# The last block of the scan: statistics in its last chunk, the first tokens' low parts on GpSimd, the first up weights' low part on VectorE, the third gather behind the scan

## The reference

```
xn = layernorm(x)                                # 8192 tokens x 256
# recurrent layer: 8 heads, state 64, head width 64
x1 = silu(causal_conv(xn @ Wx.T)); z = xn @ Wz.T
b = x1 @ Wb.T; c = x1 @ Wc.T; dt = softplus(x1 @ Wdt.T + b_dt)
for t in tokens:                                 # the scan, per head
    state = exp(dt[t] * a) * state + dt[t] * b[t] (x) x1[t]
    y[t] = c[t] . state
y = y + d_param * x1
yn = (y - mean) / sqrt(var + eps) * gn_w + gn_b  # mean, var over tokens
s = (yn * silu(z)) @ Wout.T
# experts: 8, each takes the 1024 tokens with the highest gate
idx = top_k(softmax(xn @ Wr + br).T, 1024)
tokens = xn[idx]
mid = silu(tokens @ Wu + bu); out = mid @ W_down + b_down
ffn = scatter_add(G * out, idx)
```

## Time and profile before

| | us |
|---|---|
| median of 3 runs (1223.07 to 1223.29) | 1223.28 |
| the profiled execution's own time | 1221.26 |
| its span in the trace | 1219.4 |
| VectorE busy in the span | 951.9 (78%) |
| ScalarE busy | 684.5 (56%) |
| GpSimd busy | 792.1 (65%) |

### The profile page before, as it was taken

The page is one execution under the profiler, slowest core; times in us unless marked ns, Lnnn a source line. Parts: engine busy times, 40 slices in busy tenths (PEclk is TensorE's granted clock), DMA queues, the critical chain, the costliest instruction groups (busy, mean ns, idle before and its releaser), DMA issues.

```text
span 1219.4 us, 31280 instructions
## 1 busy us (share of the span) xinstructions
PE 1205.7 (99%) x12203; PEld 1010.9 (83%) x12203; DVE 951.9 (78%) x2027; ACT 684.5 (56%) x1401; POOL 792.1 (65%) x788
## 2 busy tenths in 40 slices
PE   9999999999999999999999999999999999999998
PEld 4666678888888888888888887898899989899998
DVE  7999977898985777777778767987777775777676
ACT  6999985555565465565555556544333332555444
POOL 4889945545555577677776758467766645576674
PEclk9999999999999999999999999999999999999999
DMA  9799764643343343443343435565544446799995
GB/s 300 252 343 347 289 236 141 113 136 122 132 139 118 136 128 121 141 130 117 134 135 122 136 123 172 175 156 97 114 87 105 85 84 130 259 319 325 333 333 166
DMA packets 112354, 214.33 MB, mean 176 GB/s; under 512 B 20432, under 2 KB 78544, under 8 KB 107600
## 3 DMA queue, kind: packets, MB, share of 16 engines
q1 hardware_dynamic: 99056, 195.04, 47.5%
q0 software_dynamic: 12288, 17.05, 8.1%
q10 hardware_dynamic: 864, 0.24, 0.1%
HBM read 131.03 MB, written 81.26 MB: 174 GB/s over the span
## 4 chain that ended last, share of the span: by engine, by line
PE 88%; DVE 5%; ACT 3%; DMA 2%; issue 1%; POOL 1%; SPq 0%; ACTq 0%; DVEq 0%
PE ps L1439 27%; PE ps L1802 11%; PE ps L2061 9%; PE ps L2295 8%; PE ps L2274 7%; PE ps L1520 4%; PE ps L1487 3%; PE ps L1546 3%; PE ps L1509 3%; PE ps L1531 2%; PE ps L1560 2%; PE ps L690 2%; PE ps L743 1%; DMA x_dram<-x 1%; PE ps L1781 1%
## 5 line engine op out<-in xcount | busy, mean ns | idle before, releaser
L1395 ACT ACTIVATE decay<-tap,ncum 128x128 f32<-128x128 f32 x344 | 105.5, 389 | 141.8 <-POOL tap L1289 141.8
L1987 POOL DMA_INDIRECT ffn_dram<-ob,idx x64 | 109.6, 1713 | 85.7 <-DVE ob L1906 71.4
L2023 ACT ACTIVATE mid<-ps,b_up 128x512 f32<-128x512 f32 x96 | 66.0, 689 | 151.2 <-PE ps L1802 139.5
L1296 POOL TENSOR_TENSOR x_lo<-x,x_hi 128x512 fp32r<-128x512 f32 x56 | 78.0, 1392 | 104.1 <-ACT x_hi L1368 104.1
L1174 DVE TENSOR_TENSOR x_dt<-ps,dt 128x512 f32<-128x512 f32 x64 | 44.3, 692 | 117.8 <-PE ps L1546 117.6
L1439 PE MATMUL ps<-x_hi,w_hi_b 128*128 128x512 f32 x240 | 99.5, 414 | 0.0
L1439 PE MATMUL ps<-x_hi,w_hi_c 128*128 128x512 f32 x240 | 99.3, 414 | 0.0
L2150 POOL TENSOR_SCALAR yc<-yc,gn_scale,gn_shift 128x512 f32<-128x512 f32 x56 | 77.2, 1390 | 31.2 <-DMA yc<-y_dram 31.2
L1439 PE MATMUL ps<-x_lo,w_hi_b 128*128 128x512 f32 x240 | 94.4, 393 | 0.0
L1439 PE MATMUL ps<-x_lo,w_hi_c 128*128 128x512 f32 x240 | 94.2, 393 | 0.0
L1439 PE MATMUL ps<-x_hi,w_lo_c 128*128 128x512 f32 x240 | 93.7, 390 | 0.0
(11 more groups left out here) (319 smaller groups left out, 4075.9 us busy)
## 6 DMA issues: line engine op xcount, KB each, us to landing
tap<-cum_dram SPq DMA_DIRECT2D x43, 512.0 KB
x_dram<-x SPq DMA_DIRECT2D x16, 1024.0 KB, 5.7
yc<-y_dram SPq DMA_DIRECT2D x16, 1024.0 KB, 6.8
y_dram<-yb SPq DMA_DIRECT2D x30, 512.0 KB
x<-x_dram SPq DMA_DIRECT2D x26, 512.0 KB, 3.8
cum_row<-cum_dram SPq DMA_DIRECT2D x21, 512.0 KB
rows_dram<-xn SPq DMA_DIRECT2D x16, 512.0 KB, 3.3
ffn_dram<-zero SPq DMA_DIRECT2D x64, 128.0 KB
```

Of the source, the lines that this page charges most:

```text
L1296: nc.gpsimd.tensor_tensor(low, raw, high, ALU.subtract).then_inc(x_lo_ready, 1)
L1395: n = nc.scalar.activation(decay[g % 2][:, h, :], cum_row[g % NR][:, row, :], ACT.Exp, bias=t.ncum[:, g, h:h + 1])
L1987: pool.indirect_dma_start(out=t.ffn_dram, out_offset=bass.IndirectOffsetOnAxis(ap=t.idx[:, e, h * HC + c:h * HC + c + 1], axis=0), in_=ob[ ...
```

## The change

It moves steps between engines and places; the arithmetic is the same, but for one more copy.

- Statistics: of the block before the last, one quarter was taken in chunk 61, one in 62 and two in 63; now all four in chunk 63, before the two `x.middle` steps.
- Token tile 0: ScalarE copies each half to `mid` too, and GpSimd (`token_lo_early(pool, 0)`) forms the low part. The first copies of tile 1 now wait for it half by half (`xg_lo_ready`), since they overwrite `mid`. ScalarE's four copies of tile 0 move ahead of `exp_rows(62)`; those of tile 1 are split, half 0 ahead of `decays(62)`, half 1 at the end of chunk 61.
- The up weights' high part moves to chunk 59 on ScalarE, and their low part from GpSimd to VectorE at the end of chunk 59.
- GpSimd: `causal(62)`, `decay_c(61)`, low part of tile 0, then `causal(63)`, `decay_c(62)`, low part of tile 1, `decay_c(63)`.
- The third gather goes from chunk 63 to the start of the expert stage on GpSimd, behind a wait for the third up slice.

```diff
--- before
+++ after
...
@@ -1164,8 +1164,6 @@
             last = g % SPAN == SPAN - 1
             if g >= LAST:
                 sums(g - 1)
-            if g == LAST + 1:
-                x.token_lo(dve, 0)
             dve.wait_ge(x_turned, g + 1)
             until(dve, y_mm, g)
             if g > LAST:
@@ -1195,14 +1193,16 @@
                 next_bits(g - 1)
             if LIST0 - 1 <= g < LIST1 - 1:
                 list_slots(g - LIST0 + 1)
-            for m in range(c, c + 1) if 0 < b < NB - 1 else ((), (0,), (1,), (2, 3))[c] if b else ():
+            for m in range(c, c + 1) if 0 < b < NB - 1 else ((), (), (), range(MT))[c] if b else ():
                 dve.wait_ge(y_ready, CH * b)
                 v.bn_stats(t.ystat[:, b - 1, m, :], yb[(b - 1) % 2][:, m, :]).then_inc(stat_done, 1)
             if SLOTS <= g < SLOTS + CH:
                 slots(c)
             elif LIST1 < g <= LIST1 + 2:
                 read_lists(g - LIST1 - 1)
-            if g == NT - 1:
+            if g == LAST - 1:
+                x.split_up_lo(dve, v, 0)
+            elif g == NT - 1:
                 for f in range(2):
                     x.middle(dve, 0, f)
 
@@ -1339,19 +1339,18 @@
             b, c = g // CH, g % CH
             if g <= LAST:
                 causal(g + 1)
-            if g % SPAN and g != LAST + 2:
+            if g % SPAN and g not in (LAST + 1, LAST + 2):
                 decay_c(g)
             if LAST - 2 <= g < LAST:
                 x.gather(pool, *x.passes[g - LAST + 2])
             elif g == LAST:
-                x.split_up_lo(pool, nc.gpsimd, 0)
                 causal(g + 2)
+                decay_c(g + 1)
+                x.token_lo_early(pool, 0)
             elif g == LAST + 1:
-                x.token_lo_early(pool)
+                causal(g + 2)
                 decay_c(g + 1)
-                causal(g + 2)
-            elif g == NT - 1:
-                x.gather(pool, *x.passes[2])
+                x.token_lo_early(pool, 1)
             if b + 2 < NB:
                 lo_part(b + 2, c)
             if b + 1 < NB:
@@ -1403,10 +1402,8 @@
             if g == 0:
                 b_part(b + 1, c)
                 exp_rows(1)
-            if g == LAST:
-                x.split_up_hi(act, 0)
-            elif g == LAST + 1:
-                x.token_hi(act, 1)
+            if g == LAST + 1:
+                x.token_hi(act, 1, (0,))
             if g + 1 < NT:
                 decays(g + 1)
             if b + 2 < NB:
@@ -1414,14 +1411,18 @@
             if b + 1 < NB:
                 if g:
                     b_part(b + 1, c)
+            if g == LAST - 1:
+                x.split_up_hi(act, 0)
+            elif g == LAST:
+                x.token_hi(act, 0)
             if b + 1 < NB and c == CH - 1:
                 c_part(b + 1, c)
             if g + 2 < NT and (g + 2) % SPAN:
                 exp_rows(g + 2)
             if b + 1 < NB and c < CH - 1:
                 c_part(b + 1, c)
-            if g == LAST:
-                x.token_hi(act, 0)
+            if g == LAST + 1:
+                x.token_hi(act, 1, (1,))
 
     @block.tensor
     def _(pe):
@@ -1717,25 +1718,29 @@
     def split_up_hi(act, g):
         act.wait_ge(up_loaded[g % 2], 32 * (g // 2 + 1))
         if g == 0:
-            act.wait_ge(t.c_ready, MT * (s.NB - 1))
+            act.wait_ge(t.b_ready, MT * (s.NB - 1))
         elif g >= 2:
             act.wait_ge(up_mm, NH * FT * GS * (g - 1))
         nc.scalar.activation(up_hi[g % 2][:, :, :], up_raw[:, :, :], ACT.Copy).then_inc(up_hi_ready, 1)
 
     def split_up_lo(eng, engine, g):
         eng.wait_ge(up_hi_ready, g + 1)
+        if g == 0:
+            eng.wait_ge(t.c_ready, MT * (s.NB - 1))
         engine.tensor_tensor(up_lo[g % 2][:, :, :], up_raw[:, :, :], up_hi[g % 2][:, :, :].bitcast(F32),
                              ALU.subtract).then_inc(up_lo_ready, 1)
 
-    def token_hi(act, u):
+    def token_hi(act, u, parts=range(KT)):
         if u == 0:
             act.wait_ge(t.c_ready, MT * (s.NB - 1))
-        for k in range(KT):
+        for k in parts:
             act.wait_ge(turned, KT * u + k + 1)
+            if u == 1:
+                act.wait_ge(xg_lo_ready, k + 1)
             if u >= 2:
                 act.wait_ge(up_mm, FT * (u - 1))
             n = nc.scalar.activation(xg_hi[u % 2][:, k, :], ps_t(u)[k][:, :], ACT.Copy)
-            if u == 1:
+            if u < 2:
                 n = nc.scalar.activation(mid[k], ps_t(u)[k][:, :], ACT.Copy)
             n.then_inc(xg_hi_ready, 1)
 
@@ -1745,11 +1750,10 @@
             nc.vector.tensor_tensor(xg_lo[u % 2][:, k, :], ps_t(u)[k][:, :], xg_hi[u % 2][:, k, :].bitcast(F32),
                                     ALU.subtract).then_inc(xg_lo_ready, 1)
 
-    def token_lo_early(pool):
-        pool.wait_ge(xg_lo_ready, KT)
+    def token_lo_early(pool, u):
         for k in range(KT):
-            pool.wait_ge(xg_hi_ready, KT + k + 1)
-            nc.gpsimd.tensor_tensor(xg_lo[1][:, k, :], mid[k], xg_hi[1][:, k, :].bitcast(F32),
+            pool.wait_ge(xg_hi_ready, KT * u + k + 1)
+            nc.gpsimd.tensor_tensor(xg_lo[u][:, k, :], mid[k], xg_hi[u][:, k, :].bitcast(F32),
                                     ALU.subtract).then_inc(xg_lo_ready, 1)
 
     def middle(dve, u, f):
@@ -1775,7 +1779,9 @@
         q = u % NG
         pe.wait_ge(gathered[q], 16 * HC * (u // NG + 1))
         for k in range(KT):
-            if u:
+            if u == 1:
+                pe.wait_ge(xg_hi_ready, k + 1)
+            elif u:
                 pe.wait_ge(xg_lo_ready, KT * (u - 1) + k + 1)
             for c in range(HC):
                 mm = pe.transpose(ps_t(u)[k][:, c * P:(c + 1) * P], xg[q][:, c, k * P:(k + 1) * P], t.ident)
@@ -1989,6 +1995,8 @@
                         ap=t.idx[:, e, h * HC + c:h * HC + c + 1], axis=0),
                     in_=ob[q][:, c, :], in_offset=None, compute_op=ALU.add).then_inc(added[q], 16)
 
+        pool.wait_ge(x.up_mm, FIRST + 1)
+        x.gather(pool, *passes[2])
         pool.wait_ge(t.zero_stored, 16 * s.NT)
         for u in range(1, len(passes)):
             if u + x.NG - 1 < len(passes):
```

More of the change, by code:

```diff
@@ L939, in phase_scan @@
         sem(f"b_{n}") for n in ("row", "exp", "mix", "ymm", "smm", "y", "state"))
-    t.c_ready, t.g_ready, t.c_dec_ready, t.y_ready, t.x_turned, t.dx_ready, t.stat_done = (
-        c_ready, g_ready, c_dec_ready, y_ready, x_turned, dx_ready, stat_done)
+    t.b_ready, t.c_ready, t.g_ready, t.c_dec_ready, t.y_ready, t.x_turned, t.dx_ready, t.stat_done = (
+        b_ready, c_ready, g_ready, c_dec_ready, y_ready, x_turned, dx_ready, stat_done)
     t.lists_read, t.zero_stored, t.y_stored = lists_read, zero_stored, y_stored
```

## The result

The changed kernel takes 1226.94 us (median of 9 runs, 1226.27 to 1227.35), the kernel before, measured with it, 1223.07 (9 runs, 1220.92 to 1223.91). The medians lie 3.9 us apart; the ratio, formed over all the runs, is 1.0036, interval 1.0028 to 1.0044, which is 4.4 us slower, between 3.4 and 5.4. The forecast was +4.2 us and 1227.5.

What follows compares the result with a forecast made beforehand. In the last block, a VectorE–TensorE loop (5.28 us) bounds, with a second ScalarE–GpSimd loop that the change makes bind. Terms -0.68 + 0.85 + 1.73 + 2.28 = +4.18 us take median 1223.28 to 1227.5; range +3.9 to +4.5.

Steps and rivals of the forecast that it cites:

- x_dt 61 without the low parts: Chunk 61: with tile 0's low parts off VectorE, x_dt 61 starts earlier, a gain of 0.68 us.
- state part 61 waits for c_dec: TensorE, chunk 61: the state part waits for GpSimd's c_dec 61 until 757.31, +0.85 us.
- state part 61 to own part 62 (decays 62): Chunk 62: late decays 62 on ScalarE hold mix 62, so own part 62 starts at 763.64; +1.73 us.
- state part 62 waits for c_dec: TensorE, chunk 62: c_dec 62 behind mask 63 holds the state part until 766.61, +2.28 us.
- own part 63 to the third up slice: TensorE, end of scan: distance taken as before, so the third up slice shifts by the same 4.18 us; 0 added.
- steps 2 to 4: ScalarE–GpSimd chain, mask 62 to c_dec 62: delays pass on through copies and decays, state part 62 +4.18 us.
- step 1: Chain start: nothing moves up to decays 61's end; copies start at 750.69, exp_rows 62 moves to 752.78.
- +0.5 as its bound: GpSimd's scaling beside VectorE's up_lo: SBUF contention taken as 0, with +0.5 us kept for the range.
- VectorE's cover of 0.8 us: End of chunk 59: up_lo done at 746.3, VectorE idle until 747.14, cover left 0.8 us, cost 0.
- I take 0, with 0.3 us as the upper end: Chunk 63: four statistics put 1.2 us before the first middle steps; cost to TensorE 0, at most 0.3 us.
- The third rival: Low parts or late statistics cost more: contention +0.5, VectorE late in first expert pass +0.3; +5.0 us, 1228.3; chance 0.2.
- A TensorE gap behind 775 us: Sign of being wrong: TensorE's gap coming behind 775 us; forecast was a 2.3 us wait before chunk 62's state part.

Runs made afterwards that it cites:

- orders: Changed kernel with tile 0 copies behind exp_rows 62, first tile 1 copies behind decays 62, c_dec 62 ahead of mask 63, statistics as before; 0.9993 to before.
- after_again: The changed kernel once more, unaltered, timed and profiled a second time; ratio to the kernel before 1.0035.
- orders_scores_late: Kernel `orders` with TensorE's scores of chunks 61 to 63 behind the transposes and all four statistics in chunk 63; ratio to before 1.0006.
- cdec_first: Changed kernel with one GpSimd pair swapped in chunk 61: c_dec of chunk 62 ahead of the mask of chunk 63; ratio to before 1.0037.
- up_only: Kernel before with only the up weights moved (high part in chunk 59, low part on VectorE at its end); ratio to before 1.0000.

## Why the prediction was right

The path from own part 60 to the end, term by term, from the two profiles of the changed kernel. Each term is its distance there less the same distance before:

| term | forecast | first profile | second |
|---|---|---|---|
| x_dt 61 without the low parts | -0.68 | -0.68 | -0.68 |
| state part 61 waits for c_dec | +0.85 | +1.32 | +1.76 |
| state part 61 to own part 62 (decays 62) | +1.73 | +1.61 | +1.61 |
| state part 62 waits for c_dec | +2.28 | +2.35 | +2.36 |
| state part 62 to own part 63 | 0 | +1.32 | +0.02 |
| own part 63 to the third up slice | 0 | -0.97 | -0.98 |
| gap in the expert passes | 0 | +0.74 | +0.64 |
| sum | +4.18 | +5.69 | +4.73 |

The spans of the profiled executions differ by 6.1 and 5.6 us; 0.1 and 0.3 of that arise ahead of own part 60, and 0.3 and 0.6 stand in no term. By timing it is 4.4 and 4.3. The forecast of the median, 1227.5, was met (1226.94), that of the profiled execution, 1225.4, was not (1227.35 and 1226.86). Both were the same 4.18 us, added to a median and to a profile that lie 2.0 us apart, so how near the median came is in part luck.

- *The chain* (steps 2 to 4) is right link by link: four copies take 1.91 us (forecast 2.09), mask to c_dec 1.75, the copy of tile 1 waits for GpSimd's first half, decays 62 stand 1.11 behind it, c_dec 62 behind mask 63. The handoff from GpSimd to TensorE is 0.14 us and not 0.03. The intervention `orders` shows that these orders are the cause, and not the steps themselves.
- *State part 61* was mis-sized: +1.3 to +1.8 against +0.85. What failed is step 1, "nothing on this chain moves up to the end of decays 61": counted from own part 60, the copies started 0.56 and 1.00 us later than exp_rows 62 had before. The forecast took the contention on SBUF as 0, with +0.5 as its bound. In `after_again` the scaling took 2.24 us and mask 61 started at 747.83, 0.6 us behind the time at which ScalarE's exp_rows 61 (ended 747.03, and 0.21) had freed it. That term should have been taken, not kept for the range. The first profile has 0.5 more too, though its mask was on time; there TensorE was earlier against ScalarE by that much than in the profile before, whose chunk 59 had a pause of 0.38 us. VectorE's cover of 0.8 us was used up as well: up_lo ran from 745.14 to 747.34, and yb started at 747.26.
- *Statistics and cover.* "I take 0, with 0.3 us as the upper end" failed: 0.4 to 1.0 us in all six profiles that have them in chunk 63 with the changed order. The lead of TensorE that I read at 781.14 did not cover it: in the first profile the gap stands ahead of an up slice, in the other five ahead of a down matmul, which waits for one of three output banks. The third rival had named the down matmuls. A TensorE gap behind 775 us was also a sign of being wrong, and it came, beside the waits that were forecast. With the mended order `orders_scores_late` has the late statistics and no such gap; there TensorE waits 0.77 us for the gather first. That the statistics' removal from 61 and 62 gains 0 was right.
- *The clock* was no term at all. It fell in 5 of the 7 profiles with the changed order of these steps (all but `after_again` and `cdec_first`) and in none of the other seven, and cost 1.3 us where it can be read alone. By the timed runs above it falls in the kernel before too, only less often.
- *Own part 63 to the third up slice* was taken as before, 2.25 us. But before's profile has a pause there, which `up_only` shows again, longer (2.82 us):

```profile
767.71 1.05 PE L1531 MATMUL ps<-c_dec,state 64*64 64x128 f32 x15
769.03 0.30 PE L1531 MATMUL ps<-c_dec,state 64*64 64x128 f32 x1 [0.28 <-issue]
```

  In the others it is 1.27. So the profile before holds 1 us that the changed kernel's do not, and it hides 1 us of loss in the sum. Whether it is chance is not shown: `up_only` is the one variant whose TensorE program is that of the kernel before, and each of the two has one profile.
- *The up weights' move and the gather* cost nothing that timing can tell, as forecast, apart from the contention above.

So the sum came out near because two terms that were left out (late statistics, contention) and one that comes and goes (the clock) are partly balanced by a pause in the profile before that I had not looked for. The main terms, 1.61 and 2.35 against 1.73 and 2.28, are right for their own reasons.

## What to carry to other kernels

When two engines hand work back and forth, count a moved step on the *loop* of both, not on the engine's busy time: here each stood idle for more than 4 us at a stretch and the kernel was slower. Put what others wait for (c_dec, exp_rows) ahead of what may be late (copies, low parts), above all where a single buffer makes one engine wait for the other. And before costing a stage from one profile, look for pauses put down to "issue" on its path, since the next profile may not have them.

## What the hardware showed that I had not expected

- TensorE's granted clock fell to 0.50 (1.2 GHz) for 3.4 to 6.8 us of the last block in five of the seven profiles with the changed order, in which TensorE's longest single wait was 2.15 us. The same kernel kept 1.00 in a second profile (`after_again`, with TensorE busy 1.14 of 4.00 us between 764 and 768), and `orders` kept it through a pause of 1.90 us. At the lower clock state part and scores took 1.13 and 1.54 us and not 0.65 and 0.85.
- A GpSimd step of 0.70 us took up to 2.25 behind a VectorE subtraction of two SBUF tiles (1.75 us alone), a gather's issue of 0.95 us took 2.48, and that subtraction took up to 2.20 where a GpSimd step or issue ran when it started. Not every issue does this: in `cdec_first` one had started 0.25 us ahead of the subtraction, and the two took 0.95 and 1.76.
